# Block-wise gather and scatter by a token table in a mixture of experts, and its combine moved into the next attention layer

## The reference, cut to what matters

```python
# layer 0, feed-forward
logits = einsum('gsd,de->gse', router_input, router_logits)
choices = the two largest logits of each token                 # k = 2
sorted_xs = x_flat[xs_indices]                                 # tokens in the order of their expert
gate_out = ragged_dot(sorted_xs, w_gate, group_sizes)          # 512 -> 2 x 512, weights of the token's expert
activation = gelu(gate_out[:, 0, :]) * gate_out[:, 1, :]
expert_outputs = ragged_dot(activation, linear, group_sizes)   # 512 -> 512
expert_outputs *= per_expert_scale[expert]
out = expert_outputs[back in token order] weighted by combine_weights, summed over k
x = x + out
# layer 1, cross-attention (16 heads of 32) on _layernorm(x)
q = _ln((x @ Wq + bq), qn_w, qn_b)       # by head
k = _ln(y_main @ Wk + bk, kn_w, kn_b)    # by head; 16 "dca" rows have keys and values of their own
k_dca = _ln(y_dca @ Wkv_dca + bkv_dca, kn_dca_w, kn_dca_b)
ctx = attn(q, k, v) + attn(q, k_dca, v_dca);   out = ctx @ Wo + bo
```

## Time and profile before

| | |
|---|---|
| median of three runs | 4128.56 us |
| time of the profiled execution | 4123.47 us |
| its span, first to last instruction | 4121.7 us |
| PE busy | 3594.2 us, 87% |
| DVE, ACT, POOL busy | 2434.8, 1463.5, 1088.5 us |
| mean granted clock of PE | 0.944 |

### The profile page before, as it was taken

One profiled execution on the slowest core, in us unless ns is written; L12 is line 12 of the kernel. 1 busy time (PEld: TensorE's weight loads), 2 busy tenths in 40 slices (PEclk: granted clock), 3 DMA queues, 4 the chain that ended last, 5 costly groups with the idle time before them and its releaser, 6 DMA issues.

```text
span 4121.7 us, 59149 instructions
## 1 busy us (share of the span) xinstructions
PE 3594.2 (87%) x23070; PEld 2735.2 (66%) x23070; DVE 2434.8 (59%) x4704; ACT 1463.5 (36%) x3121; POOL 1088.5 (26%) x1065
## 2 busy tenths in 40 slices
PE   6999999938988936999799979999779999999875
PEld 5888888823444423555599845555468999999854
DVE  6777777741122244777544345666556777777658
ACT  2333333321100003555222225555235555555421
POOL 0000000030020057665222225665422222222211
PEclk9999999969999968999899989999989999999987
DMA  2111100023533230000110000000000000000001
GB/s 90 39 43 39 38 14 9 1 92 140 195 115 137 82 92 36 5 6 5 52 42 31 1 34 3 3 3 4 14 26 16 16 16 17 16 17 6 1 14 41
DMA packets 66180, 160.09 MB, mean 39 GB/s; under 512 B 9200, under 2 KB 33392, under 8 KB 59376
## 3 DMA queue, kind: packets, MB, share of 16 engines
q1 hardware_dynamic: 60784, 139.53, 9.9%
q0 software_dynamic: 5120, 16.78, 1.2%
HBM read 217.10 MB, written 34.60 MB: 61 GB/s over the span
## 4 chain that ended last, share of the span: by engine, by line
PE 35%; DVE 7%; issue 3%; POOL 2%; ACT 2%; DMA 1%; SPq 0%; DVEq 0%; POOLq 0%; ACTq 0%
PE banks L93 31%; PE banks L184 4%; DVE cWK L2471 1%; DVE cm L2469 1%; ACT P L67 1%; POOL rs L76 1%; DVE XL L76 0%; DVE xn L81 0%; POOL kst L76 0%; POOL X L76 0%; DVE X L76 0%; DVE st L222 0%; DVE PL L76 0%; DVE P L80 0%; ACT nkT L70 0%
## 5 line engine op out<-in xcount | busy, mean ns | idle before, releaser
L76 DVE TENSOR_TENSOR X<-X,banks 128x512 f32<-128x512 f32 x352 | 240.1, 683 | 158.9 <-PE banks L93 158.4
L93 PE MATMUL banks<-WB,exsT 128*128 x624 | 294.7, 627 | 32.1 <-DVE exsT L73 31.8
L87 DVE TENSOR_REDUCE nmx<-banks 128x4 f32<-128x1024 f32 (+2 forms) x256 | 239.0, 955 | 127.5 <-PE banks L93 123.4
L93 PE MATMUL banks<-XH,wqh 128*128 128x256 f32 x1024 | 292.7, 286 | 0.0
L93 PE MATMUL banks<-XH,wql 128*128 128x256 f32 x1024 | 286.1, 279 | 0.0
L93 PE MATMUL banks<-XL,wqh 128*128 128x256 f32 x1024 | 286.0, 279 | 0.0
L93 PE MATMUL banks<-XH,tT 128*128 128x256 f32 x1024 | 246.6, 283 | 13.4 <-issue 6.6
L93 PE MATMUL banks<-XL,tT 128*128 128x256 f32 x1024 | 245.4, 282 | 0.0
L93 PEld LDWEIGHTS banks<-WB,exsT 128*128 128x128 f32 x624 | 121.5, 200 | 182.9 <-issue 182.9
L67 ACT ACTIVATE nPT<-banks 128x1024 f32<-128x1024 f32 x192 | 195.8, 1020 | 108.5 <-PE banks L93 106.5
L184 PE MATMUL banks<-ident,xn 128*128 128x128 f32 x448 | 87.0, 332 | 162.7 <-DVE xn L81 135.1
(11 more groups left out here) (350 smaller groups left out, 10356.8 us busy)
## 6 DMA issues: line engine op xcount, KB each, us to landing
WB<-in_moe_w SPq DMA_DIRECT2D x39, 3072.0 KB
rows_in<-zero SPq DMA_DIRECT2D x4, 2496.0 KB, 11.7
exs<-rows_in SPq DMA_DIRECT2D x39, 256.0 KB, 2.7
rows_out<-eos SPq DMA_DIRECT2D x39, 256.0 KB, 2.1
wqr<-in_L_xattn_Wq SPq DMA_DIRECT2D x16, 512.0 KB, 3.6
wor<-in_L_xattn_Wo SPq DMA_DIRECT2D x16, 512.0 KB, 4.6
eraw<-in_L_ffn_factors SPq DMA_DIRECT2D x7, 1024.0 KB, 5.0
X<-in_x SPq DMA_DIRECT2D x4, 1024.0 KB, 9.0
```

The source lines that it names most:

```text
L76: return self.e.tensor_tensor(out, a, b, op)
L87: return self.e.tensor_reduce(out, a, AX.X, op, **kw)
L93: return self.e.matmul(out, l, r, start=start, stop=stop, skip_group_check=skip)
```

## The change

The memory tensor `rows_in` now holds the 2048 normed rows in token order: SP writes them with 16 plain DMAs as they come out of the norm, and the zero fill is gone. From the positions DVE and PE make tables by block: with row = position mod 128 and block = position / 128, OS is the one-hot of the row, OB that of the block (40 wide), OT is OB times the number of the (choice, token) pair, OW is OB times the gate. 32 accumulating matmuls OS x OT give for each of 128 rows and 40 columns the pair's number (`row`; 0 for padding) and from it the token (`tok`); 32 more, OS x OW, give the gate value. In "rows" POOL gathers a block's 128 rows by `tok`; in "lower" DVE multiplies the result by its gate and POOL scatters it by `row` to `rows_out`, which is now in (choice, token) order with one spare row for padding. Combine and second norm leave the expert stage. They are steps of layer 1's list: "gl" (SP loads both rows of a tile with one plain DMA, POOL adds the first), "ga" (DVE adds the second and takes the statistics, POOL the rsqrt), "gn" (norm), "gt" (turn on PE bank 7, copy by ACT). XF of this layer holds 8 tiles instead of 16. The three centrings of "dcen" give way to a subtraction of the mean from the dca keys themselves. All places of layer 1 are new.

```diff
 block_steps:  yield "upper", 0
+        yield "gates", 0
 sp_experts:
+        for t in range(NT):
+            sp.wait_ge(S["xn"], ln_at(1, t))
+            sp.dma(self.XS[128 * t:128 * t + 128, :], w["XN"][:, t, :]).then_inc(S["kept"], 16)
 ...
                 if j == 2:
-                    sp.wait_ge(S["scatter"], 512)
+                    sp.wait_ge(S["pe_one"], ONE["ewt"])
 ...
-            if step == "rows":
-                sp.wait_ge(S["scatter"], 512)
-                sp.wait_ge(S["xs_turned"], j - 2)
-                sp.dma(w["xs"][:, j % 3, :], self.XS[128 * j:128 * j + 128, :]).then_inc(S[f"xs{j % 3}"], 16)
-            if step == "lower":
-                sp.wait_ge(S["os"], j + 1)
-                sp.dma(self.OS[128 * j:128 * j + 128, :], w["os"][:, j % 2, :]).then_inc(S[f"os{j % 2}"], 16)
 pool_experts:
-        for t in range(NT):
-            for k in range(2):
-                pool.e.indirect_dma_start(self.XS, bass.IndirectOffsetOnAxis(w["POS"][:, k, t:t + 1], 0), w["XN"][:, t, :],
-                                          None).then_inc(S["scatter"], 16)
+        pool.wait_ge(S["dve_one"], ONE["eob"])
+        pool.tt(w["OT"][:], w["OB"][:], number, ALU.mult).then_inc(S["pool_one"], 1)
+        pool.wait_ge(S["dve_one"], ONE["tokens"])
+        pool.wait_ge(S["kept"], 16 * NT)
         for step, j in self.block_steps():
+            if step == "rows":
+                pool.wait_ge(S["xs_turned"], j - 2)
+                pool.e.indirect_dma_start(w["xs"][:, j % 3, :], None, self.XS, bass.IndirectOffsetOnAxis(w["tok"][:, j:j + 1], 0)
+                                          ).then_inc(S[f"rows{j % 3}"], 16)
+            if step == "lower":
+                pool.wait_ge(S["back"], 16 * j)
+                pool.wait_ge(S["os"], j + 1)
+                pool.e.indirect_dma_start(self.OS, bass.IndirectOffsetOnAxis(w["row"][:, j:j + 1], 0), w["os"][:, j % 2, :],
+                                          None).then_inc(S["back"], 16)
 ...
-            if t + 3 < NT:
-                self.pool_gather(pool, t + 3)
-            if t >= 1:
-                self.pool_ln(pool, 2, t - 1)
 pe_experts:
+        for i in range(2 * NT):
+            m = pe.mm(banks[3][:, 0:40], w["OS"][:, i, :], w["OT"][:, i, :], i == 0, i == 2 * NT - 1)
 ...
+            if step == "gates":
+                pe.wait_ge(S["dve_one"], ONE["eow"])
+                for i in range(2 * NT):
+                    m = pe.mm(banks[7][:, 0:40], w["OS"][:, i, :], w["OW"][:, i, :], i == 0, i == 2 * NT - 1)
 dve_experts:
+        dve.tt(w["OB"][:], w["jio"][:].unsqueeze(1).to_broadcast([128, 2 * NT, 40]), column, ALU.is_equal).then_inc(S["dve_one"], 1)
+        for i in range(2 * NT):
+            m = dve.ts(w["OS"][:, i, :], w["io"][:], pb[:, 0, i:i + 1], None, ALU.is_equal)
 ...
-                dve.copy(w["os"][:, j % 2, :], banks[6 + j % 2][:]).then_inc(S["os"], 1)
+                dve.ts(w["os"][:, j % 2, :], banks[6 + j % 2][:], w["gate"][:, j:j + 1], None, ALU.mult).then_inc(S["os"], 1)
 PLACES[1] (those that moved most, and the new ones):
-            "ksc": -44.5, "qp": (-62.5, -61.5), "kp": -55.5, "kb": -55.5, "dcen": -54.5, "dv": -42, "dk": -41
+            "ksc": -60.5, "qp": (-62, -61.5), "kp": -72.5, "kb": -72, "dv": -71.5, "dk": -68,
+            "gl": -96.5, "ga": -83, "gn": -77, "gt": -77.5
 sp_narrow:
+            if step == "gl":
+                sp.wait_ge(S["gsum"], 3 * (a - 2) + 1)
+                sp.dma(w["gt"][:, a % 2, :, :], back[a]).then_inc(S[f"x{2 + a % 2}"], 16)
 pool_narrow:
+            if step == "gl":
+                pool.wait_ge(S[f"x{2 + t % 2}"], 16 * (t // 2 + 2))
+                pool.tt(x, x, w["gt"][:, t % 2, 0, :], ALU.add).then_inc(S["gadd"], 1)
+            if step == "ga":
+                pool.wait_ge(S["var"], ln_rs(2, t))
+                self.rsqrt(pool, self.rs[:, t:t + 1], self.sc1[:, t:t + 1]).then_inc(S["rs"], 1)
 dve_narrow:
+            if step == "ga":
+                dve.wait_ge(S["gadd"], t + 1)
+                dve.tt(x, x, w["gt"][:, t % 2, 1, :], ALU.add).then_inc(S["gsum"], 1)
+                dve.e.bn_stats(...); dve.e.bn_aggr(...); dve.ts(sc1, variance + 1e-5)
+            if step == "gn":
+                dve.wait_ge(S["rs"], ln_rs(2, t))
+                dve.ts(w["xn"][:, t % 2, :], self.X[:, t, :], self.mv[:, t, 0:1], self.rs[:, t:t + 1],
+                       ALU.subtract, ALU.mult).then_inc(S["xn"], 1)
 sp_program:
         self.fence(sp, 2)
+        self.sp_narrow_load(sp, 1)
+        sp.wait_ge(S["back"], 16 * NBLK)
```

More of the change, by code:

```diff
@@ L879, in expert_tiles @@
         sb("sm", [128, 12, NT], F32)
-        sb("POS", [128, 2, NT], I32)
+        sb("tok", [128, 40], I32)
+        sb("row", [128, 40], I32)
+        sb("gate", [128, 40], F32)
         sb("e8", [128, 6, 8], F32)
         sb("n8", [128, 8], I32)
-        sb("jio", [1, 40], F32)
+        sb("jio", [128, 40], F32)
         w["ge"] = self.at("ege", [1, 40, 8], F32, self.xl_at + 30720)
@@ L906, in expert_tiles @@
         work("tri", [128, 128], F32)
-        w["gt"] = self.at("egt", [128, 4, 2, 512], F32, base)
+        work("io", [128, 128], F32)
+        work("tid", [128, 2, NT], F32)
+        work("pf", [128, 2, NT], F32)
+        work("pi", [128, 3, 2 * NT], I32)
+        work("pb", [128, 2, 2 * NT], F32)
+        work("tf", [128, 40], F32)
+        w["OS"] = self.at("eOS", [128, 2 * NT, 128], F32, base + 49152)
+        for i, n in enumerate(("OB", "OT", "OW")):
+            w[n] = self.at("e" + n, [128, 2 * NT, 40], F32, base + 65536 + 5120 * i)
         self.W["e"] = w
@@ L954, in sp_experts @@
         sp.wait_ge(S["fsum"], 16)
-        for i in range(4):
-            sp.wait_ge(S[f"gather{i}"], 128)
     def pool_experts(self, pool):
@@ L1229, in dve_experts @@
         dve.copy(EI[:, 2, :], r0(3)).then_inc(S["dve_one"], 1)
+        tab = banks[3][:, 0:40]
+        dve.wait_ge(S["pe_one"], ONE["etab"])
+        rt(dve.copy(w["row"][:], tab))
+        a = rt(dve.ts(w["tf"][:], tab, 1.0, 0.0, ALU.subtract, ALU.max))
+        dve.wait_ge(S["rt"], a)
+        a = rt(dve.copy(w["tok"][:], w["tf"][:]))
+        dve.wait_ge(S["rt"], a)
+        dve.e.tensor_scalar(w["tok"][:], w["tok"][:], T - 1, None, ALU.bitwise_and).then_inc(S["dve_one"], 1)
+        dve.wait_ge(S["load_b"], ONE["esc"])
+        for k in range(2):
+            a = rt(dve.tt(tm[:], oh[:, k, :, :], w["esc"][:].unsqueeze(1).to_broadcast([128, NT, 8]), ALU.mult))
+            dve.wait_ge(S["rt"], a)
+            a = rt(dve.red(sm[:, 11, :], tm[:], ALU.add))
+            dve.wait_ge(S["rt"], a)
+            a = rt(dve.tt(sm[:, 6 + k, :], sm[:, 6 + k, :], sm[:, 11, :], ALU.mult))
+        dve.wait_ge(S["rt"], a)
+        dve.wait_ge(S["dve_one"], ONE["eob"])
+        gates = sm[:, 6:8, :].rearrange("p k t -> p (k t)").unsqueeze(2).to_broadcast([128, 2 * NT, 40])
+        dve.tt(w["OW"][:], w["OB"][:], gates, ALU.mult).then_inc(S["dve_one"], 1)
         for step, j in self.block_steps():
@@ L1246, in dve_experts @@
                 dve.wait_ge(S["down"], j + 1)
-                dve.wait_ge(S[f"os{j % 2}"], 16 * (j // 2))
-                dve.copy(w["os"][:, j % 2, :], banks[6 + j % 2][:]).then_inc(S["os"], 1)
+                dve.wait_ge(S["back"], 16 * (j - 1))
+                dve.ts(w["os"][:, j % 2, :], banks[6 + j % 2][:], w["gate"][:, j:j + 1], None, ALU.mult).then_inc(S["os"], 1)
+            if step == "gates":
+                dve.wait_ge(S["pe_one"], ONE["ewt"])
+                rt(dve.copy(w["gate"][:], banks[7][:, 0:40]))
+                dve.wait_ge(S["rt"], count[0])
             if step == "factor" and j >= 2:
@@ L1377, in narrow_tiles @@
         if l1:
+            for i, (n, shape) in enumerate((("XF", [128, 4, 1024]), ("gt", [128, 2, 2, 512]), ("xn", [128, 2, 512]))):
+                w[n] = self.at("n" + n, shape, F32, self.xh_at + (0, 16384, 24576)[i])
             side("OT", [128, 2, 4, 256], F32)
@@ L1701, in pe_narrow @@
             if step == "ln":
-                self.pe_ln(pe, 2 if l1 else 4, t)
-                self.wait_xt(pe, 2 if l1 else 4, t)
+                self.pe_ln(pe, 4, t)
+                self.wait_xt(pe, 4, t)
+            if step == "gt":
+                self.wait_turned(pe, L, w["before7"][step, t])
+                pe.wait_ge(S["xn"], ln_at(2, t))
+                for a in range(4):
+                    m = self.turn(pe, banks[7][:, 128 * a:128 * a + 128], w["xn"][:, t % 2, 128 * a:128 * a + 128])
+                m.then_inc(S["ln_turned"], 1)
             if step in ("dv", "dk"):
@@ L1822, in act_narrow @@
             if step == "ln":
-                self.act_ln(act, 2 if l1 else 4, t)
+                self.act_ln(act, 4, t)
+            if step == "gt":
+                if t >= 8:
+                    act.wait_ge(S["n_loq"], max(w["stack"]["q", (t - 8, hh)] for hh in range(2)) + 1)
+                act.wait_ge(S["ln_turned"], ln_at(2, t))
+                act.acopy(self.queries(L, t), z7).then_inc(S["xh"], 1)
```

190 lines of the change are left out of this document (94 added, 96 removed), and 9 rows, old and new, of the table PLACES.

## The result

| | before | after |
|---|---|---|
| median of 4 runs | 4129.81 us (4123.03 to 4131.49) | 4063.34 us (4057.60 to 4065.45) |
| ratio | | 0.984, 95% interval 0.9823 to 0.9857 |
| profiled execution, its span | 4123.47, 4121.7 us | 4062.26, 4060.5 us |
| granted TensorE clock, mean | 0.944 | 0.953 |
| bytes moved by DMA | 160.09 MB | 145.68 MB |

A forecast was written before the change was run, and what follows sets the result against it. PE, busy 87%, was taken as the limit except around the block start and the border, where POOL bounds the attention's start. Start -14.5, loop -20, border -54, attention +12 sum to -76.5 us: median 4052, range 4022 to 4092.

The forecast's parts named there:

- Case (a): Whole kernel: the forecast itself, a median of 4052 us; chance 0.60.
- Start of the blocks: Before the expert blocks: 32 scatters go, two tables and a gather replace them; -14.5 us.
- The race with the weights: Start of the blocks: first weights arrive at 919.0 against the rows' path at 920, so both end at 920.
- Loop: The 39 expert blocks: gathers on POOL's queue remove most waits for rows; -20 us, bounds -5 to -25.
- 7.9 is under 9: Block loop: gathers beside weights land in 7.9 us (scatters' median), within the about 9 us they are issued ahead.
- 1.5 us ahead of the weights, because SP first loads three values: Block loop: POOL issues the gather some 1.5 us before SP issues the expert weights.
- Rival (d): Block loop: gathers late for every block; gain gone at 11.3 us landing, 4233 us at 14; chance 0.04.
- the 7.3 us of slower blocks: Block loop: blocks after a wait for rows run slower, 7.3 us over six, counted in the 24.7 recoverable.
- Border: Combine, second norm and start of layer 1's attention: POOL is the limit; -54 us, bounds -65 to -41.
- Attention: Layer 1's steady attention: PE stays the limit, about eleven tiles pay 1.1 us each for the norm; +12 us.
- if a tile of the attention takes 24: Steady attention: sign that the forecast is wrong; it expected 22 to 23 us a tile.
- In lists of fixed order with DVE at 86% some waits must come: Steady attention: waits beyond PE's sure 0.6 us a tile, hence 1.1 us a tile taken.

The follow-up runs named there:

- experiment 3: Changed kernel with gate and token tables made by one set of 32 matmuls of 80 columns, scale factors applied earlier; 4063.19 us.
- experiments 1 and 5: First: changed kernel with POOL's gather issued ahead of the scatter, 4058.37 us. Second: that plus DVE's factor additions moved behind the copy ehT, 4030.76 us.
- experiment 7: Changed kernel with each of the 4 transposes of the second norm made twice in the attention; 4071.12 us.
- experiment 8: Changed kernel with the statistics of the second norm taken twice on DVE in the attention; 4066.78 us.
- experiment 9: Changed kernel with the old places for most steps of layer 1's attention, gather steps and projections keeping their new places; 4143.38 us.
- experiments 4 and 8: First: changed kernel with gathered rows of tiles 0 and 1 loaded ahead of layer 1's biases and weights, 4060.88 us. Second: norm statistics taken twice, 4066.78 us.
- experiment 12: Changed kernel with gather first, factor additions behind ehT, one 80-column table, early row loads, split comparisons, products on DVE and 44 matmuls of ones; 4006.70 us.
- experiment 10: Kernel before the change, with SP issuing the rows of block j+3 ahead of that block's expert weights; 4116.44 us.

## Why the prediction was right, and where its terms were off

**The whole.** Faster, inside the range, 11 us above the point. Case (a) is what happened. Three of its terms promised 29 us too much in all, the fourth 16 too little, and these errors partly cancelled: that the point came this close is in part luck.

**Start of the blocks: -8.6, not -14.5.** The path was the one listed. Mis-sized: the comparisons (4.8 forecast, 8.46 measured: 0.2 us each instead of 0.15, and 2.2 us of a stop by POOL's product, which I had counted as running beside them); the first table (11, measured 13.84); the second (7.6, measured 8.97). For the first table I had assumed that the clock rises on the way; it stayed at 0.50, and experiment 3 shows that its columns are not what it pays. The second I had put at its price at the full clock; the clock fell within it. The race with the weights did not bind: they are in by 921.5, and PE waits for the rows until 925.42.

**Loop: -7.6, not -20.** The step that failed is "7.9 is under 9": a median was set against a limit that the six slowest gathers had to keep. They landed in 10.5 to 12 us (9.2 of cover plus waits of 1.34 to 2.75); the seventh beside weights took 9.5 and had 11.5 of cover. With it failed "1.5 us ahead of the weights, because SP first loads three values": SP no longer waits for os, and the weights left 0.8 us ahead of the gather. Rival (d) had priced this mechanism and was right that only blocks beside 3 MB of weights would show it. And the 7.3 us of slower blocks, which I hung on these waits, belonged in part to the factor additions that the waits had covered; experiments 1 and 5 separate them.

**Border: -42.9, not -54.** From the last down step: 25.6 us to the first addition (22.7 forecast), 67.0 to the last stack of tile 1 (62), 8.3 to the first score (4); together the 12.2 us by which 100.9 exceeds the 88.7 of the forecast. In the first part the fence took 6.55 us, not 5.43, and the load stood behind the 11 others, as said. In the second POOL's busy time was nearly right (50 forecast, 51.6 measured), its idle time was not 12 but 15.4. What the forecast lacked is that POOL does not bound this chain alone: PE's projections lie in it, at 0.70 to 0.88 of the clock, and POOL's idle time follows them (64.3 us from the first addition to that stack at a clock of 0.88, 67.0 at 0.76, 72.8 and 73.4 at 0.70, for the same work on POOL). In the third part the stack is followed by one more transposed tile and query projection on PE (1541.63, 3.62 us), which my 4 us, copied from before, did not have.

**Attention: -4.0, not +12.** The tile was mis-sized first: 21.7 us is not a period, a tile takes 24.3. So my sign of being wrong, "if a tile of the attention takes 24", came true and means nothing: the kernel before takes 24.3 as well. The norm's cost on PE is real (0.44 us a tile, experiment 7), and DVE is off the path as said (experiment 8). The step that failed is "In lists of fixed order with DVE at 86% some waits must come": the diff also moved most of the other steps of this list ("all places of layer 1 are new" was too much: the scores "s" and the output projection "out" kept theirs), PE's idle time in seven tiles fell from 4.9 to 3.4 us, and its work rose by 1.7 where I had 4.2. I had read the new places only to order POOL's queue at the border. The 4 us less come at the end (from the ninth output projection of the attention to the sixteenth and last 119.1 us before, 115.2 after); that new places in the tail do this is argued, not shown.

**What stays open:** how much of the attention's +77 in experiment 9 comes from which place; what lowers PE's clock at the border in experiments 4 and 8; and what the moved places, without the norm, would give the kernel before.

## What to carry to other kernels

A transfer that is hidden by a fixed cover must be judged by its slowest landings in that place, not by a median; and when a wait is removed, look for the other one that it covered in the same blocks. Here the two cheapest edits (ask for the rows before the other transfer, add the factor matrix where PE is busy) gave half as much as the whole change, with it (32.6 us) or without it (32.4). In an order written out by hand the new places are part of the change: what they are worth has to be priced, or at least read, with the operations.

## What the runs showed of the hardware

- DVE and POOL stop each other on SBUF tiles: one 128x128 comparison of DVE lasted 2.39 us (the others came 0.2 apart) while POOL multiplied 128x1280; POOL's product took 6.45 instead of 2.34 us beside DVE's 4.42 us comparison of 128x4096.
- 64 fp32 matmul records with a new 128x128 weight tile each took 13.84 us with 40 columns and 13.91 with 80.
- PE was busy without a gap in that table, and its clock stayed at 0.50, the lower of its two levels (1.2 GHz). In the second table of the same form the clock was 1.00 at the start and fell to 0.50 after 5.2 us, when PE had been busy without a gap for 14 us; in experiment 12, which leaves that table out, it stayed at 1.00 there.
- Of 39 gathers of 256 KB the seven beside 3 MB of weights landed in 9.5 to 12 us, the fastest other one in 3.2. Issued a block earlier, ahead of the weights, the six that had been waited for landed in 3.4 to 6.0 us, and others beside the weights took up to 11.8.
- PE could start an upper step 0.5 to 0.6 us after the last packet of its weights had ended (experiment 10, four times).
